# Masked cross attention: the keys of two batches projected beside the first experts, and only one token tile taken through the queries before the first maxima

## The chip, the cores and the metric

The kernel runs on one core of one Trainium2 chip. A core has TensorE (PE, matrix products), VectorE (DVE), ScalarE (ACT), GpSimd (POOL) and SyncE (SP, which here issues all transfers). The metric is the device time of one launch in microseconds; less is better.

## The reference, cut to what matters

The program is a stack of seven layers over 16 batches of 64 tokens with 128 channels. The change touches the border of the third (experts, `_L0_ffn_ref`) and the fourth (`_L1_xattn_ref`), whose first half is cross attention of 16 heads of 8 channels over 1601 context rows per batch, with an additive mask per batch and key:

```python
def _mha(x, ctx, mask, qw, qb, kw, kb, vw, vb):
    q = _split_heads(x @ qw + qb)
    k = _split_heads(ctx @ kw + kb)
    v = _split_heads(ctx @ vw + vb)
    scores = jnp.einsum('bqhd,bkhd->bhqk', q, k) / np.sqrt(D // H).astype(np.float32)
    if mask is not None:
        scores = scores + mask
    probs = jax.nn.softmax(scores, axis=-1)
    out = jnp.einsum('bhqk,bkhd->bqhd', probs, v)
...
x = x + _L0_ffn_ref(_layernorm(x, axis=-1), L0_ffn_gate, ...)
x = x + _L1_xattn_ref(_layernorm(x, axis=-1), ctx_1024, mask_Bx1x1xS2_ff0, ...)
```

The queries need `x` after the experts. Keys and values need only `ctx_1024` and the weights.

## The kernel before

Each engine has its own instruction list, written out by hand in the order in which it runs, and the lists meet at semaphores. `progress(name, steps)` makes a semaphore with named steps; `P[name].done(ins, step)` raises it, `at(engine, name, step, i)` waits for it. Every product is recorded at line 264, every tile transpose of a layer norm at line 294.

**The experts.** The first mixture of experts is a hardware loop `e0` of four iterations, two experts each. Per iteration `moe_tensor` issues for n = 0 to 3 (expert j, token half t) four steps `h` (two sums of three products of 512 columns each) and, one n later, a step `y` (16 products of 128 columns). ACT applies Silu (line 646), DVE multiplies (line 662) and adds `y` into `x` (line 667). The steps `h` use PSUM banks 0 to 3, `y` banks 4 and 5; banks 6 and 7 are free in the loop. At the start of an iteration PE waits for `wcol` (line 655), which DVE writes after the last sum.

**From the experts to attention.** After the loop DVE takes the layer norm of `x` (`ln_all_vector(3)`: statistics, variance, then 8 tiles of 128 tokens at line 277); POOL computes the reciprocal root `rstd` (line 283), behind two memsets of the value areas (lines 968 and 969). PE transposes 8 tiles and projects queries for all 1024 tokens. The queries are kept as a high and a low part, `qh` and `ql`, which lie in the same memory as `kh` and `kl`, the parts of the keys. SP copies `qh`, `ql`, `qh` into every fourth partition of `QS` (line 924). POOL spreads `QS` per batch into `QB` (line 978). Keys of a batch are projected in four chunks (512, 512, 512, 65 columns), all through PSUM bank 7: product on PE, high part on ACT (line 1081), low part on DVE (line 1493), then the next chunk. SP copies `kh`, `kh`, `kl` and the mask into the stack `KS` of that batch (lines 865, 872).

**The slots.** `slots` runs slot n = -2 to 16, each of 13 steps k. In slot n batch n has its scores and exponentials (`s`, line 1094) and weighted values, batch n+1 its values and the maxima m3 to m12 (scores over a wide tile, `maximum` on PE and a reduction on DVE, lines 1508 and 1510), batch n+2 its keys and, at k = 10 to 12, its maxima m0 to m2. `SIDES` and `MAX_STEPS` (lines 1623, 1624) say what stands at which k. Two pairs of PSUM banks take the maxima in turn. After m12 the negated maximum `nm` is transposed, split and sent by SP into `QB` (line 877, `nm_stacked`), and the batch's scores wait for that. So before slot 0 the slots -2 and -1 hold: keys of batch 0, maxima m0 to m2 of batch 0; then keys of batch 1, values of batch 0, maxima m3 to m12 of batch 0, m0 to m2 of batch 1.

## Time and profile before

| what | value |
|---|---|
| median of 3 runs | 1282.2 us (1277.72 to 1285.16) |
| the profiled execution | 1281.95 us, of it span from the first to the last instruction 1280.2 us |
| mean granted TensorE clock | 0.889 of full speed |
| PE / DVE / ACT / POOL busy | 1022.1 / 657.4 / 483.0 / 196.8 us |
| last sum of the experts | 379.4 us |
| first scores of batch 0 | 454.55 us |

The span is what the trace shows. The trace names an instruction by line, tile written and tiles read, its start and its length, and what ended the idle time before it. "PEld" is the loading of weights, "SPq" SP's issue of a transfer. A 32-bit product shows as two records, a product of `F32R` tiles as one.

### The profile page before, as it was taken

The page shows a single profiled execution, that of the slowest core. Times are in us where ns is not written, and L with a number is a line of the kernel's source. Part 1 is how long each engine was busy: PE and PEld are TensorE (multiplying, and loading weights), DVE is VectorE, ACT ScalarE, POOL GpSimd, SP SyncE. Part 2 cuts the span into 40 slices and gives each one's busy share as a digit, 9 for nine tenths or more (in the row PEclk, how much of TensorE's full clock was granted, in tenths as well). Part 3 has the DMA queues.
Part 4 walks back from the last instruction along what each step waited for, and adds up shares of the span by engine and source line. Part 5 has one row for each costly group of instructions (what it writes and reads, how often), then busy time and mean ns, then how long its engine had stood idle before and what let it go on. Part 6 is the DMA issues. An engine that isn't in the chain of part 4 may idle for free.

```text
span 1280.2 us, 22033 instructions
## 1 busy us (share of the span) xinstructions
PE 1022.1 (80%) x9278; PEld 731.4 (57%) x9278; DVE 657.4 (51%) x1131; ACT 483.0 (38%) x622; POOL 196.8 (15%) x178
## 2 busy tenths in 40 slices
PE   3687777899873699999999999999658634848888
PEld 2355456787761266666666666666436412547776
DVE  4133655343343556666666676664166367763111
ACT  0234332222232146666666656666304200402333
POOL 2000430211212001111111111110141013200110
PEclk9799887999996579999999999999877766859999
DMA  8585000101201333333333333330000100001110
GB/s 278 187 314 207 2 1 1 50 25 43 83 0 53 141 123 108 111 130 110 107 107 108 139 137 123 108 108 18 1 1 2 33 0 1 2 0 34 34 33 17
DMA packets 41349, 98.52 MB, mean 77 GB/s; under 512 B 9976, under 2 KB 24960, under 8 KB 41264
## 3 DMA queue, kind: packets, MB, share of 16 engines
q1 hardware_dynamic: 41264, 97.29, 22.1%
q8 instruction: 65, 1.06, 0.3%
q14 instruction: 20, 0.16, 0.0%
HBM read 55.50 MB, written 0.73 MB: 44 GB/s over the span
## 4 chain that ended last, share of the span: by engine, by line
PE 61%; DVE 16%; ACT 8%; issue 5%; SPq 4%; DMA 3%; POOL 3%; DVEq 0%; POOLq 0%; ACTq 0%
PE PS L264 57%; DVE kl L1493 3%; ACT kh L1081 3%; ACT PT L1094 3%; DVE prT L1497 2%; SPq L896 2%; PE PS L357 2%; DVE mx L1508 2%; DMA ctxT<-in_ctx_T 1%; PE PS L294 1%; POOL rstd_all L283 1%; DVE x L667 1%; DVE u_all L277 1%; DMA work_area<-in_ctx_T 1%; DVE stats_all L269 1%
## 5 line engine op out<-in xcount | busy, mean ns | idle before, releaser
L1508 DVE TENSOR_REDUCE mx<-PS 128x2 f32<-128x1024 f32 x192 | 230.7, 1217 | 85.1 <-PE PS L264 85.0
L1094 ACT ACTIVATE PT<-PS 128x1024 f32<-128x1024 f32 (+1 forms) x208 | 212.4, 1021 | 95.2 <-PE PS L264 94.0
L264 PE MATMUL PS<-QB,QS 128*128 128x512 f32 x576 | 159.4, 425 | 23.7 <-DVE wcol L655 21.7
L264 PE MATMUL PS<-QB,KS 128*128 128x256 f32 (+1 forms) x832 | 166.8, 323 | 9.2 <-ACT PT L1094 8.5
L264 PEld LDWEIGHTS PS<-QB,QS 128*128 128x128 f32 x576 | 110.3, 202 | 60.7 <-issue 26.8
L264 PEld LDWEIGHTS PS<-QB,KS 128*128 128x128 f32 (+1 forms) x832 | 116.5, 187 | 43.5 <-issue 31.8
L264 PE MATMUL PS<-PT,work_area 128*32 128x128 f32 (+1 forms) x3328 | 135.3, 281 | 0.5 <-ACT PT L1094 0.5
L264 PE MATMUL PS<-KS,QB 64*128 64x512 f32 (+1 forms) x512 | 110.8, 462 | 13.1 <-DMA KS<-kl 9.5
L667 DVE SCALAR_TENSOR_TENSOR x<-PS,wcol,x 128x128 f32<-128x128 f32 x128 | 44.9, 351 | 138.1 <-PE PS L264 134.7
L264 PE MATMUL PS<-nat_area,work_area 128*128 128x128 f32 (+2 forms) x1312 | 100.8, 261 | 17.2 <-DVE work_area L662 5.9
L264 PEld LDWEIGHTS PS<-nat_area,work_area 128*64 128x64 f32 (+1 forms) x1312 | 96.3, 165 | 31.3 <-ACT work_area L395 12.3
L264 PEld LDWEIGHTS PS<-PT,work_area 128*32 128x32 f32 (+1 forms) x3328 | 78.8, 109 | 46.5 <-issue 43.2
L646 ACT ACTIVATE work_area<-PS 128x512 f32<-128x512 f32 x64 | 38.3, 598 | 127.7 <-PE PS L264 127.7
L294 PE MATMUL PS<-consts,u_all 128*128 128x128 f32 x64 | 15.7, 426 | 86.6 <-DVE u_all L277 66.0
L264 PE MATMUL PS<-ctxT,w_L_xattn_ck_w 128*128 128x512 f32 (+1 forms) x128 | 66.8, 607 | 21.3 <-DVE kl L1493 17.5
L264 PE MATMUL PS<-w_L_xattn_cv_w,ctxT 128*128 128x128 f32 (+1 forms) x416 | 78.7, 311 | 0.0
L264 PEld LDWEIGHTS PS<-KS,QB 64*128 64x128 f32 x512 | 46.2, 193 | 48.9 <-issue 14.5
L1081 ACT ACTIVATE kh<-PS,c_L_xattn_ck_b 128x512 fp32r<-128x512 f32 x64 | 38.1, 595 | 86.0 <-PE PS L264 71.7
L264 PEld LDWEIGHTS PS<-w_L_xattn_cv_w,ctxT 128*128 128x128 f32 (+1 forms) x416 | 55.8, 194 | 23.3 <-issue 22.8
L1493 DVE SCALAR_TENSOR_TENSOR kl<-PS,c_L_xattn_ck_b,kh 128x512 fp32r<-128x512 f32 x64 | 40.5, 633 | 51.4 <-ACT kh L1081 51.3
L294 PEld LDWEIGHTS PS<-consts,u_all 128*128 128x128 f32 x64 | 12.5, 223 | 88.5 <-DVE u_all L277 41.0
L978 POOL TENSOR_TENSOR QB<-QS,consts 128x1024 fp32r<-128x1024 f32 x16 | 31.2, 1955 | 202.1 <-PE PS L264 186.0
(237 smaller groups left out, 1255.5 us busy)
## 6 DMA issues: line engine op xcount, KB each, us to landing
KS<-kh SPq DMA_DIRECT2D x32, 800.5 KB
ctxT<-in_ctx_T SPq DMA_DIRECT2D x24, 800.5 KB, 4.4
nat_area<-in_ctx_tiles SPq DMA_DIRECT2D x16, 832.0 KB, 6.6
KS<-kl SPq DMA_DIRECT2D x16, 800.5 KB
work_area<-in_ctx_T SPq DMA_DIRECT2D x8, 800.5 KB, 10.2
nat_area<-in_L_ffn_experts_w SPq DMA_DIRECT2D x24, 256.0 KB, 3.3
nat_area<-in_L_ffn_W SPq DMA_DIRECT2D x16, 256.0 KB, 3.0
KS<-mask_parts SPq DMA_DIRECT2D x32, 50.1 KB
```

Of the source, the lines that this page charges most:

```text
L264: return T.matmul(o, l, r, start=start, stop=stop, **k)
L294: last = T.transpose(PS[:, 512 * (6 + h) + 128 * t:512 * (6 + h) + 128 * t + 128], src[:, 4 * h + t, :], ident)
L357: last = T.transpose(PS[:, o:o + 128], L["pr"][:, 128 * b:128 * b + 128], ident)
L646: ins = S.activation(g_act[:, c % 2, :], bank(2 * (c % 2)), ACT.Silu)
L667: last = V.scalar_tensor_tensor(x[:, 4 * t + q, :], PS[:, 512 * (4 + t) + q * 128:512 * (4 + t) + (q + 1) * 128], wcol[:, j, 4 * t + q:4 * ...
L896: sp.dma_start(dst, src).then_inc(loads, 16)
L978: P["qb_g"].done(G.tensor_tensor(QB[b % 3][:, :].rearrange("p (g h q) -> p g h q", g=4, h=4), QS[:, :, SEQ * b:SEQ * b + SEQ].unsqueeze(2) ...
L1081: P["keys_a"].done(S.activation(kh[:, c0:c0 + cw], bank(7, cw), ACT.Identity, bias=COLS["L1_xattn_ck_b"][:, 0:1]), f"kh{c}")
L1094: P["exp_a"].done(S.activation(PT[0:rows, par, :], PS[0:rows, 1024:2048], ACT.Exp), f"e{k}")
L1493: P["keys_v"].done(V.scalar_tensor_tensor(kl[:, c0:c0 + cw], bank(7, cw), COLS["L1_xattn_ck_b"][:, 0:1], kh[:, c0:c0 + cw], ALU.add, ALU.s ...
L1497: P["sum_v"].done(V.reciprocal(rsum, rsum), "sum")
L1508: ins = V.reduce_max(by_pair[:, :, j // 3, j % 3:j % 3 + 1], src, AX)
```

## The change

Five things are done together.

1. **Keys in the loop.** The keys of batches 0 and 1 are projected in `e0`: 401 columns of each batch per iteration, overlapping by one column, behind step h(1, 0) for batch 0 (bank 6) and behind h(3, 0) for batch 1 (bank 7). Their contexts are loaded once the first self attention has read its tiles. Batch 1 gets parts of its own, in the early half of `nat_area`. SP stacks both behind the loop's weight loads (`stack_keys`).
2. **Values of batch 0** are projected right behind the loop, into banks 2 to 5.
3. **One tile of queries.** Only token tile 0 (batches 0 and 1) is normalised, transposed and projected first; its 128 columns go into `QS`, and the maxima of batch 0 follow. `qh` and `ql` lie in `small` and in `QB[2]`.
4. **Slots -2 and -1** keep only maxima and `nm`. The seven other tiles, and their queries, come between slot -1 and slot 0 (`q1`, `q2`); `QB` of batch 2 waits for them.
5. **Fillers.** POOL writes only the 16 one-columns of each value group, behind `rstd`; ACT fills `QS` first and `KS[2]` after `KS[1]` is stacked; `L1_xattn_co_b` is added to `u_all` on POOL.

```diff
-        qh, ql = kh[:, 0:TOKENS], kl[:, 0:TOKENS]
+        KH = [kh, nc.alloc_sbuf_tensor_at("kh1", [128, KPAD], F32R, offset=nat_at)]
+        KL = [kl, nc.alloc_sbuf_tensor_at("kl1", [128, KPAD], F32R, offset=nat_at + 4 * 1608)]
...
+        def early_keys_tensor(b, i):
+            T.wait_ge(ctxT_loaded[b], 16)
+            P["pk_p"].done(mm(bank(6 + b, KW), W["L1_xattn_ck_w"][:, :], ctxT[:, b, bass.ds((KW - 1) * i, KW)]), f"b{b}")
+
+        def early_keys_scalar(b, i):
+            at(S, "pk_p", f"b{b}", i)
+            P["pk_a"].done(S.activation(KH[b][:, bass.ds((KW - 1) * i, KW)], bank(6 + b, KW), ACT.Identity,
+                                        bias=COLS["L1_xattn_ck_b"][:, 0:1]), f"b{b}")
+
+        def early_keys_vector(b, i):
+            at(V, "pk_a", f"b{b}", i)
+            P["pk_v"].done(V.scalar_tensor_tensor(KL[b][:, bass.ds((KW - 1) * i, KW)], bank(6 + b, KW),
+                                                  COLS["L1_xattn_ck_b"][:, 0:1], KH[b][:, bass.ds((KW - 1) * i, KW)],
+                                                  ALU.add, ALU.subtract), f"b{b}")
+
+        def early_keys(keys, i):
+            return {(1, 0): lambda: keys(0, i), (3, 0): lambda: keys(1, i)}
...
+            if n < 0:
+                return [item for item in SIDES[k] if item == "nm" and n == -1]
...
+            moe_sync(sp, "e0", (A["L0_ffn_experts_w1"], A["L0_ffn_experts_w3"], A["L0_ffn_experts_w2"], None), first_contexts)
             sp.wait_ge(mask_saved, 32)
+            sp.wait_ge(stacks_ready, 2)
             for b in range(2):
-                load_context(b)
-            at(sp, "q3_v", "ql")
-            sp.wait_ge(stacks_ready, 4)
+                stack_keys(b)
+            at(sp, "q3_v", "ql0")
+            sp.wait_ge(stacks_ready, 3)
             for k, src in enumerate((qh, ql, qh)):
-                sp.dma_start(QS[k:128:4, :, :].bitcast(F32), src.bitcast(F32)).then_inc(qs_stacked, 16)
+                sp.dma_start(QS[k:128:4, :, 0:128].bitcast(F32), src[:, 0:128].bitcast(F32)).then_inc(qs_first, 16)
+            at(sp, "vals_p", "v2", 0)
+            load_context(2)
+            sync_slot(-1)
+            at(sp, "q3_v", "ql2")
+            for k, src in enumerate((qh, ql, qh)):
+                sp.dma_start(QS[k:128:4, :, 128:TOKENS].bitcast(F32), src[:, 128:TOKENS].bitcast(F32)).then_inc(qs_stacked, 16)
             slots(sync_slot)
...
-            G.memset(VA[0], 1.0).then_inc(consts_ready, 1)
-            G.memset(VA[1], 1.0).then_inc(consts_ready, 1)
             ln_all_gpsimd(3)
-            g.wait_ge(qs_stacked, 16 * 3)
+            for va in VA:
+                G.memset(va[:, :, :, 16:32], 1.0).then_inc(consts_ready, 1)
+            g.wait_ge(qs_first, 16 * 3)
...
+            def queries(j, lo, hi, src, tmp):
+                at(V, "q3_p", f"q{j}")
+                vdone(V.tensor_scalar(tmp, src, COLS["L1_xattn_cq_b"][:, 0:1], HD ** -0.5, ALU.add, ALU.mult), "q3_v", f"qf{j}")
+                vdone(V.tensor_copy(qh[:, lo:hi], tmp), "q3_v", f"qh{j}")
+                vdone(V.tensor_tensor(ql[:, lo:hi], tmp, qh[:, lo:hi], ALU.subtract), "q3_v", f"ql{j}")
+
+            ln_stats_vector(3, x)
+            ln_apply_vector(x, u_all, range(3))
+            at(V, "q3_p", "T0")
+            P["q3_v"].done(V.tensor_copy(xT_all[:, 0:128], bank(6, 128)), "x0")
+            ln_apply_vector(x, u_all, range(3, 5))
+            queries(0, 0, 128, bank(0, 128), prT[:, 512:640])
+            ln_apply_vector(x, u_all, range(5, PAIRS))
+            slot(-2)
+            slot(-1)
...
+            queries(1, 128, 512, bank(7, 384), prT[:, 512:896])
+            queries(2, 512, 1024, bank(6), prT[:, 512:1024])
             slots(slot)
```

In the rows of order below a name is that of the tile (written<-read), and the brackets name the semaphores waited for. First PE inside the loop, from the second group h(0, 2) on, as it was:

```order
L264 MATMUL PS<-QB,QS 128x512 [waits e0_v]
L264 MATMUL PS<-QB,QS 128x512 x5
L264 MATMUL PS<-nat_area,PT 128x128 [waits e0_v]
L264 MATMUL PS<-nat_area,PT 128x128 x15
L223 REGISTER_ALU
```

and as it is now, from the end of h(1, 0) to step y of n = 0:

```order
L270 MATMUL PS<-QB,QS 128x512 x5
L270 ISA [waits ctxT_loaded0]
L270 MATMUL PS<-ctxT,w_L_xattn_ck_w 128x401
L226 REGISTER_ALU
L270 MATMUL PS<-QB,QS 128x512 [waits e0_v]
L270 MATMUL PS<-QB,QS 128x512 x5
L270 MATMUL PS<-nat_area,PT 128x128 [waits e0_v]
```

One product of 401 columns stands between two steps `h`; the only wait that comes with it is that for the context.

PE behind the loop, before:

```order
L294 MATMUL PS<-consts,u_all 128x128 [waits ln_normalised,consts_ready,e0_v]
L294 MATMUL PS<-consts,u_all 128x128 x7
L264 MATMUL PS<-xT_all,w_L_xattn_cq_w 128x512 [waits ln_copied] x2
L264 MATMUL PS<-ctxT,w_L_xattn_ck_w 128x512 [waits ctxT_loaded0]
L264 MATMUL PS<-ctxT,w_L_xattn_ck_w 128x512 [waits keys_v] x2
L264 MATMUL PS<-ctxT,w_L_xattn_ck_w 128x65 [waits keys_v]
L264 MATMUL PS<-KS,QB 128x512 [waits ks_stacked0,qb_g]
```

and now:

```order
L270 MATMUL PS<-w_L_xattn_cv_w,ctxT 65x128 [waits e0_v]
L270 MATMUL PS<-w_L_xattn_cv_w,ctxT 128x128 x12
L1299 MATMUL PS<-consts,u_all 128x128 [waits ln_normalised]
L270 MATMUL PS<-xT_all,w_L_xattn_cq_w 128x128 [waits q3_v]
L270 MATMUL PS<-KS,QB 128x512 [waits qb_g,consts_ready,ks_stacked0,vals_a,q3_v]
```

The keys are gone from between the queries and the first maxima; 13 value products stand ahead of the one transpose.

PE from the end of the maxima m0 to m2 of batch 1 to the first scores (`QB,KS`), now; before, the scores followed directly on a value product and no tile or query stood here:

```order
L270 MATMUL PS<-KS,QB 128x512 [waits max_v]
L270 MATMUL PS<-KS,QB 128x512
L1402 MATMUL PS<-consts,u_all 128x128 [waits ln_normalised]
L1402 MATMUL PS<-consts,u_all 128x128 x2
L1405 MATMUL PS<-consts,u_all 128x128 x4
L270 MATMUL PS<-xT_all,w_L_xattn_cq_w 128x384 [waits ln_copied]
L270 MATMUL PS<-xT_all,w_L_xattn_cq_w 128x512 [waits ln_copied]
L270 MATMUL PS<-QB,KS 128x256 [waits nm_stacked]
```

Seven transposes and two query products now come between the last maximum and the first scores.

## Rows read from the trace of the kernel before

**Rows 1.** Head of the page.
```profile
span 1280.2 us, 22033 instructions
```

**Rows 2.** Windows: span, busy us (instructions) PE, PEld, DVE, ACT, POOL; clock, DMA share, GB/s.
```profile
379.40:424.20 44.80, 10.58 (x22) 4.57 (x22) 15.12 (x37) 11.42 (x6) 13.88 (x6) 0.61 0.26 93
424.20:454.50 30.30, 25.90 (x73) 13.06 (x73) 20.37 (x22) 4.41 (x8) 0.00 (x0) 0.50 0.24 84
454.50:480.30 25.80, 25.41 (x243) 16.60 (x241) 15.78 (x18) 14.80 (x19) 0.00 (x0) 0.87 0.38 132
480.30:506.00 25.70, 25.08 (x282) 16.48 (x281) 18.29 (x17) 15.84 (x22) 4.10 (x5) 1.00 0.37 131
```

**Rows 3.** Chain that ended last, in order: start us, us, what.
```profile
382.35 2.83 POOL work_area L969
...
398.19 4.62 DMA QS<-kh
...
406.70 2.09 PE PS L264 x2
...
416.31 7.74 DMA KS<-kl
```

**Rows 4.** Timeline from the loop's end to the first key: start us, us, engine, instruction.
```profile
379.62 1.64 DVE L269 BATCH_NORM_STATS2 stats_all<-x 128x6 f32<-128x128 f32 x8 [0.21 <-DVE x L667]
...
381.97 0.40 DVE L274 TENSOR_SCALAR var_all<-mv_all 128x8 f32<-128x8 f32 x1
...
385.14 1.63 POOL L283 TENSOR_TENSOR rstd_all<-var_all,consts 128x8 f32<-128x8 f32 x1
386.81 2.14 DVE L277 TENSOR_SCALAR u_all<-x,mv_all,rstd_all 128x128 f32<-128x128 f32 x8 [4.44 <-POOL rstd_all L283]
...
390.29 1.48 DVE L288 COPY xT_all<-PS 128x512 f32<-128x512 f32 x2 [1.34 <-PE PS L294]
...
391.03 2.93 PE L264 MATMUL PS<-xT_all,w_L_xattn_cq_w 128*128 128x512 f32 x4
...
395.59 1.23 DVE L1535 TENSOR_TENSOR kl<-PT,kh 128x1024 fp32r<-128x1024 f32 x1
...
402.84 0.69 ACT L1081 ACTIVATE kh<-PS,c_L_xattn_ck_b 128x512 fp32r<-128x512 f32 x1 [14.35 <-DMA QS<-kh]
402.88 6.58 POOL L978 TENSOR_TENSOR QB<-QS,consts 128x1024 fp32r<-128x1024 f32 x3 [16.11 <-DMA QS<-kh]
```

**Rows 5.** Timeline, maxima of batch 0 up to the first scores.
```profile
424.19 1.22 PE L264 MATMUL PS<-KS,QB 64*128 64x512 f32 x4 [9.53 <-DMA KS<-kl]
...
441.88 4.75 DVE L1508 TENSOR_REDUCE mx<-PS 128x2 f32<-128x1024 f32 x4
...
442.27 1.23 PE L264 MATMUL PS<-w_L_xattn_cv_w,ctxT 128*128 128x128 f32 x4
...
447.27 0.71 DVE L1510 TENSOR_REDUCE mx<-PS 128x8 f32<-128x528 f32 x1 [0.65 <-PE PS L264]
...
449.05 0.28 DVE L1501 TENSOR_TENSOR nml<-PS,nmh 8x128 fp32r<-8x128 f32 x1
...
454.55 1.22 PE L264 MATMUL PS<-QB,KS 128*128 128x256 f32 x4
```

**Rows 6.** Timeline inside the expert loop, last product of an iteration.
```profile
330.36 3.83 PE L264 MATMUL PS<-nat_area,work_area 128*128 128x128 f32 x32 [1.49 <-DVE work_area L662]
```

**Rows 7.** Groups by form, 229.5 to 379 us: name xcount, busy us, mean ns, idle.
```profile
L646 ACT ACTIVATE work_area<-PS 128x512 f32<-128x512 f32 x54 | 32.3, 598 | 111.1 <-PE PS L264 111.1
```

**Rows 8.** Windows of 1 us, for the granted clock (third column from the end).
```profile
389.00:390.00 1.00, 0.90 (x5) 0.94 (x6) 0.00 (x0) 0.00 (x0) 0.00 (x0) 0.50 0.00 0
...
393.00:394.00 1.00, 1.00 (x4) 0.52 (x3) 0.75 (x1) 0.00 (x0) 0.00 (x0) 1.00 0.00 0
...
450.00:451.00 1.00, 0.92 (x3) 0.52 (x4) 0.02 (x1) 0.12 (x1) 0.00 (x0) 0.50 0.02 4
...
461.00:462.00 1.00, 1.00 (x6) 0.59 (x4) 0.00 (x0) 0.33 (x1) 0.00 (x0) 0.88 0.00 0
```

More of the change, by code:

```diff
@@ L651, in moe_scalar, with moe_vector @@
                 beside.get((n, c), lambda: None)()
-        def moe_vector(name, gated, i, first=lambda: None):
+        def moe_vector(name, gated, i, first=lambda: None, beside={}):
             for j in range(2):
@@ L711, in build @@
         T_loaded = [sem(f"T_loaded{q}") for q in range(2)]
-        progress("q3_p", ["q0", "q1"])
-        progress("q3_v", ["qf0", "qf1", "qh", "ql"])
+        progress("q3_p", ["T0", "q0", "q1", "q2"])
+        progress("q3_v", ["x0"] + [f"{part}{j}" for j in range(3) for part in ("qf", "qh", "ql")])
+        progress("pk_p", ["b0", "b1"])
+        progress("pk_a", ["b0", "b1"])
+        progress("pk_v", ["b0", "b1"])
         CS = range(len(CHUNKS))
@@ L792, in slots @@
         def slots(slot):
[L794 removed]
+            for n in range(BATCH + 1):
                 slot(n)
+        KW = 401
+        def early_keys_tensor(b, i):
[12 more added lines that the diff above has]
+            return {(1, 0): lambda: keys(0, i), (3, 0): lambda: keys(1, i)}
         def maxima(n, k):
@@ L822, in bank7_free @@
         def bank7_free(n, k):
-            before = [(m, item) for m in range(-2, n + 1) for i in range(KT) for item in closed(sides(m, i))
+            before = [(m, item) for m in range(n + 1) for i in range(KT) for item in closed(sides(m, i))
                       if (m, i) < (n, k) and item != "nm"]
+            if not before:
+                at(nc.tensor, "q3_v", "ql1")
             if before:
@@ L1287, in slot @@
                             pe.wait_ge(nm_stacked, 32 * (n + 1))
+                        if n == 0 and k == 1:
+                            at(T, "q3_v", "ql2")
                         if k >= 1:
@@ L1309, in slot @@
                         maximum(b, j)
+            slot(-2)
+            slot(-1)
+            pe.wait_ge(ln_xn, 4 * PAIRS)
+            for t in range(1, 4):
+                last = T.transpose(PS[:, 3584 + 128 * (t - 1):3584 + 128 * t], u_all[:, t, :], ident)
+            last.then_inc(ln_T, 1)
+            for t in range(4, 8):
+                last = T.transpose(PS[:, 3072 + 128 * (t - 4):3200 + 128 * (t - 4)], u_all[:, t, :], ident)
+            last.then_inc(ln_T, 1)
+            pe.wait_ge(ln_xT, 7)
+            P["q3_p"].done(mm(bank(7, 384), W["L1_xattn_cq_w"][:, :], xT_all[:, 128:512]), "q1")
+            pe.wait_ge(ln_xT, 8)
+            P["q3_p"].done(mm(bank(6), W["L1_xattn_cq_w"][:, :], xT_all[:, 512:1024]), "q2")
             slots(slot)
```

125 lines of the change are left out of this document (79 added, 46 removed).

## The prediction

> **What bounds the kernel now.** I read the head of the page, then windows of the stretches around the change, then the chain that ended last, then the timeline. The span is 1280.2 us [rows 1]. From 454.5 us on, where the slots run, PE is busy 25.41 of 25.80 us and 25.08 of 25.70 us [rows 2]: the slots are bound by PE, and nothing that is only moved from one slot to another would pay. The two windows ahead look otherwise. From the end of the experts (379.4) to the first maximum (424.2) PE is busy 10.58 of 44.8 us, and no other engine more than 15.12; from there to the first scores (454.5) it is busy 25.90 of 30.3 us, but at half clock, 0.50 [rows 2]. So 75.1 us lie between the last sum of the experts and the first scores, and they are a chain of latencies: the chain holds a memset on POOL that runs until 385.2, 4.62 us for the last query transfer, 2.09 us for a product of one key chunk at half clock, 7.74 us for the stack of keys [rows 3]. This stretch is what the change is worth; the loop ahead of it is what it costs.
>
> I count from E, the last sum of the experts (379.4 before, later after), and follow PE to m0 of batch 0 and to the first scores. Before they stand at E+44.8 and E+75.1 [rows 5].
>
> **E to m0.** Statistics and variance are unchanged and end at E+3.0 [rows 4]. `rstd` then began only at 385.14, since POOL was filling [rows 3, 4]; now it is first on POOL and ends at E+3.0+1.63 = E+4.7. Of the eight tiles, 2.14 us together, three come before the transpose: E+5.5 [rows 4]. PE meanwhile does 13 value products. Two of them take 1.23 us at half clock [rows 5], so 13 take 8.0; at full clock I bound them by half of that, 4.0. Clock 1.0 holds in the loop and falls some time after PE stops, so I take the middle, 6.0: PE is free at E+6.1. Transpose, copy of 128 columns (0.74 us for 512 [rows 4]: at most 0.3), product of 128 columns (2.93 for 1024 [rows 4]: 0.5), three DVE operations on 128 columns instead of 1024 (the longest was 1.23 [rows 4]: at most 0.35 each, 0.9 with their waits) give `ql0` at E+8.4. The seven other normalised tiles fall partly in DVE's waits here, partly under the transfers.
>
> The three query transfers took 1.37 us (396.82 to 398.19) for two issues and 4.62 for the last, 6.0 us with 1024 columns [rows 3, 4]. With 128 columns the issues stay and the bytes are one eighth. No row has such a transfer on this path: it costs between its three issues alone, 2.1, and 6.0. I take the middle, 4.1: E+12.5. The Trainium skill's page "DMA: Bandwidth & Descriptors" (section on the fixed cost) gives a fixed 2.0 us and bytes over 436 kB per us; by it the last transfer would be seen 2.2 us after its issue and this term would be 3.6, the sum 0.5 less. No row here shows it.
>
> POOL then spreads one `QB`: 6.58 us for three, 2.2 each [rows 4]: E+14.7, and m0 at E+14.8. **Gone: 30.0 us.** Among them are the keys of batch 0 (four rounds of PE, ACT, DVE through one bank), their stack of 7.74 us, the co_b addition and two of the three `QB`. Their cover is safe: batch 0's last chunk is projected some 30 us before E, batch 1's some 12 us before, the stack needs some 9 us, and it is first wanted at E+14.8 and E+32.
>
> **m0 to the scores.** Before, `nml` of batch 0 ended at 449.33, 25.1 us after m0, since every other step waited for a key chunk of batch 1 [rows 5]. Now only maxima stand there: 0.8 for the first product, 12 reductions at 4.75/4 = 1.19, then 0.71 [rows 5], then the 1.35 us from there (447.98) to the end of `nml` [rows 5]: 17.2, so E+32.0. DVE sets the pace: two steps' products take 1.22 on PE [rows 5], 0.6 to 0.8 each with their start. **Gone: 8.0 us.** If instead each step's handover were seen (product and reduction in turn, 2.0 a step), it would be 10 more; with two pairs of banks the four reductions in a row at 1.19 speak against it.
>
> Behind it, 5.2 us passed to the scores; this grows. m0 to m2 of batch 1 need three reductions, 3.6: E+35.6. PE transposes seven tiles beside them. Then a copy of 384 columns, 0.6 (of 0.74 for 512), then q1 and q2 on PE: a 512-column product at half clock is 2.09 [rows 3], so 1.57+2.09 = 3.7, the second copy beside the first. Scores at E+39.9, 7.9 instead of 5.2: **added 2.7 us.** The `nm` transfers, issued from E+32 on, have 8 us to land where the query transfers took 6.0. Step k = 1 of slot 0 waits for `ql2`: three DVE operations of 512 columns, some 2 us, against scores of 1.22 [rows 5] and a maximum and a value product, together 1.2 to 1.5, on PE behind q2. Zero, 1 at worst. The other queries' transfers and `QB` of batch 2 are wanted at k = 10, some 25 us later; behind them on POOL and SP stand only work of slot 1 and the next mask. co_b on POOL has the same cover. ACT's fill of `KS[2]` moves behind its value copies and is wanted later still.
>
> So the scores come 75.1 - 39.9 = 35.2 us sooner, measured from E.
>
> **What the loop pays.** E itself moves. Eight products of 401 columns are added where PE has no idle time but 1.49 us an iteration ahead of the last step `y` and the wait for `wcol`. In the same loop 16 products of 128 columns of the same type take 3.83 us [rows 6], 0.24 each; 401 columns are 0.75. Upper bound: half of the 2.09 for 512 at half clock, 1.05 [rows 3]. Eight times 0.75 is **6.0 us**, bounds 5.8 and 8.4. ACT and DVE come along, 0.55 and 0.6 us twice an iteration (the high part of 512 columns took 0.69 [rows 4], the low part a little more). ACT had 111.1 us idle in the windows of the loop, all for PE [rows 7]. DVE's low part waits for ACT's high part, and behind it in DVE's list is the product of h(n, 1), whose reader on PE stands behind a whole step `y` of 3.83 us: hidden; without `y` it would cost some 0.5 each. An Identity on ACT after Silu shows no table load in the trace: the first `kh` at 402.84 begins with the transfer it waited for [rows 4].
>
> **Sum.** 1281.95 (the profiled execution; the median of the runs shown is 0.25 above) - 35.2 + 6.0 = 1252.8. Behind the first scores nothing changes. Forecast 1253.
>
> **Rivals.**
>
> *The clock comes back sooner, 1249.* PE began a dense stretch at 389 and the clock was 1.00 at 393; another began at 450, and it was still 0.50 until 461 [rows 8]. The forecast repeats the second: seven transposes, q1, q2 and the first scores make PE dense from about E+34, and I let slot 0 lose as much as before. If it is the first, q1, q2 and the first scores run at 2.4 GHz (2.4 us less) and some 1.5 us of slot 0 come back. The Trainium skill's page "TensorE: Matmul & The Clock Gate" (section on the two states) says that the default is throttled and sustained activity releases it; by that rule the dense stretch is what counts and this rival would hold. The first case of rows 8 agrees, the second does not, with 92% busy at 450 and half clock for 11 us.
>
> *The chain keeps part of its length, 1261.* The value products all at half clock hold the transpose 2 us longer, the transfers take their full 6.0 (1.9 more), and each maximum shows 0.3 us of handover (4 more). Each is open; together they give 8 us. For it speaks that every step of the new chain is short and waits on another engine.
>
> *The first maxima wait for something else, 1268.* The change would then not do what it says. The candidate is SP's list: the query transfers stand behind the stacks of both batches. If the last stack is issued or read so late that it is still moving at E+8, its 7.74 us come ahead of the queries, and `QB` of tile 0 is late by up to that, with the other small terms about 15 us.
>
> *The loop pays more, 1264.* PE stalls behind an inserted product until ACT and DVE have taken their parts: 0.75+0.55+0.6 and two handovers of 0.1 make 2.1 us an insertion, 17 us instead of 6. Against it: no wait on PE in the loop names the early keys but the one for the context, and the reader of the next `h` stands behind `y`.
>
> *Slower than before: the clock stays at half through the first slots, 1290.* Before, the clock rose 7 us into slot 0, and slot 0 at a mean clock of 0.87 took 25.8 us against 25.7 for the next at 1.00 [rows 2]. Now slot 0 comes after a stretch in which PE does only maxima, 0.6 of each 1.19 us, with nothing between them. If PE then stayed at 0.50, a slot with 25.1 us of PE work would grow by 0 to 25 us; with the middle, 12.5, the gain of 29 is gone after 2.3 slots, and three of them give 1253+37 = 1290. For it: the clock was 0.50 over the whole of 424 to 454 with PE busy 85% [rows 2]. Against it: it did rise, 11 us after the stretch became dense [rows 8], and slots are 97% dense.
>
> **How the numbers follow.** Forecast (1248 to 1257) 0.60, clock sooner 0.13, chain longer 0.16, something else first 0.04, loop pays more 0.03, clock at half 0.03, something not named 0.01. The range reaches over the clock rival and the longer chain, with 3 us for the spread of runs: 1245 to 1266. A measurement of this kernel tells some 0.5%, 6.4 us, from no change. Of the named cases only the clock at half ends on the other side of that, and the unnamed one may end within it or a little short: faster 0.95, same 0.02, slower 0.03.
>
> **What would show it.** In the profile after: the last sum of the experts at 385 to 386; `rstd` starting within 0.2 us of the variance; the first maximum 14 to 16 us behind the last sum; reductions of batch 0 at 1.2 us each without gaps; the first scores at 425 to 426, 40 us behind the last sum; one slot still 25.7 us. The forecast is wrong if the loop lengthens by over 9 us, if the first maximum is over 20 us behind E, or if the slots lengthen.

## The result, and the profile after

| | before | after |
|---|---|---|
| median, beside one another | 1281.39 us (1277.72 to 1285.16, 4 runs) | 1241.92 us (1235.97 to 1244.09, 4 runs) |
| repeated, same chip | 1279.8 us (11 runs) | 1240.08 us (1235.66 to 1247.4, 6 runs) |
| the profiled execution, with its clock | 1281.95 us, 0.889 | 1241.52 us, 0.908 |

The ratio is 0.9684 (95% interval 0.964 to 0.9729), and 0.9693 (0.9661 to 0.9724) in the repetition. The kernel is faster, as forecast, but by 39.5 us where 29 were forecast, and 1241.92 lies below the range of 1245 to 1266.

The head of the page of after, which answers to [rows 1], and its first line on the engines:

```profile
span 1239.7 us, 22079 instructions
...
PE 1004.5 (81%) x9280; PEld 723.3 (58%) x9280; DVE 658.4 (53%) x1136; ACT 482.1 (39%) x622; POOL 195.1 (16%) x179
```

The same line of the page of before:

```profile
PE 1022.1 (80%) x9278; PEld 731.4 (57%) x9278; DVE 657.4 (51%) x1131; ACT 483.0 (38%) x622; POOL 196.8 (15%) x178
```

PE was busy 1022.1 us before and is busy 1004.5 us now, with two records more, which is one product: eight key products came into the loop, eight left the stretch behind it, and the queries are three products instead of two. A product costs PE more time at half clock; the mean clock rose from 0.889 to 0.908. So part of the gain is not a wait that went.

Windows of after, columns as in [rows 2]: nearly all of the loop, last sum (E = 379.2) to first maximum, from there to the first scores, two slots.

```profile
204.70:379.20 174.50, 157.95 (x905) 131.56 (x904) 72.61 (x142) 46.39 (x75) 27.60 (x24) 0.98 0.18 57
379.20:394.70 15.50, 4.39 (x29) 3.63 (x30) 8.21 (x29) 11.94 (x7) 6.62 (x5) 0.73 0.18 55
394.70:417.40 22.70, 16.56 (x51) 7.73 (x51) 19.95 (x22) 0.00 (x0) 3.73 (x2) 0.51 0.02 8
417.40:443.10 25.70, 23.77 (x261) 15.55 (x259) 17.97 (x24) 14.24 (x18) 2.12 (x2) 1.00 0.44 155
443.10:468.80 25.70, 25.10 (x289) 16.63 (x282) 18.77 (x19) 15.51 (x21) 4.09 (x5) 1.00 0.38 133
```

The two stretches between loop and slots were 44.8 and 30.3 us [rows 2]; they are 15.5 and 22.7 us, together 38.2 us, 36.9 less. A slot still takes 25.7 us, but the first now runs at clock 1.00, not 0.87.

The timeline of after from E to the first maximum (start, length, engine, instruction, idle before), which answers to [rows 4]:

```profile
379.23 3.12 PE L270 MATMUL PS<-w_L_xattn_cv_w,ctxT 128*65 128x128 f32 x26 [1.60 <-DVE x L681]
...
382.06 1.63 POOL L295 TENSOR_TENSOR rstd_all<-var_all,consts 128x8 f32<-128x8 f32 x1 [39.86 <-DVE var_all L280]
...
383.64 2.91 POOL L1034 MEMSET work_area<- 128x1664 f32 x2
383.73 3.21 DVE L285 TENSOR_SCALAR u_all<-x,mv_all,rstd_all 128x128 f32<-128x128 f32 x3 [1.81 <-POOL rstd_all L295]
...
386.68 0.48 PE L1299 MATMUL PS<-consts,u_all 128*128 128x128 f32 x1 [4.33 <-DVE u_all L285]
...
389.02 0.29 DVE L1626 TENSOR_TENSOR QB<-prT,q_hi 128x128 fp32r<-128x128 f32 x1
389.34 0.53 SPq L982 DMA_DIRECT2D QS<-q_hi  x1
...
392.56 3.74 POOL L1044 TENSOR_TENSOR QB<-QS,consts 128x1024 fp32r<-128x1024 f32 x2 [6.02 <-DMA QS<-q_hi]
...
394.71 1.22 PE L270 MATMUL PS<-KS,QB 64*128 64x512 f32 x4 [6.38 <-POOL QB L1044]
```

And from the last reductions of batch 0 to the first scores, which answers to [rows 5]:

```profile
409.98 0.18 DVE L1609 TENSOR_REDUCE nm<-mx 128x8 f32<-128x32 f32 x1
...
411.01 0.28 DVE L1596 TENSOR_TENSOR nml<-PS,nmh 8x128 fp32r<-8x128 f32 x1
...
415.44 2.50 PE L270 MATMUL PS<-xT_all,w_L_xattn_cq_w 128*128 128x384 f32 x4 [0.24 <-DVE xT_all L1638]
...
417.38 1.03 PE L270 MATMUL PS<-QB,KS 128*128 128x256 f32 x4
...
420.75 0.50 PE L270 MATMUL PS<-QB,KS 128*128 128x256 f32 x2 [1.54 <-DVE QB L1626]
```

**Where the 40.5 us between the two spans went.** I cut both traces at four points: start of the experts' loop (first copy to `wcol`), start of the layer norm behind it, first exponential of batch 0, first exponential of batch 15.

| stretch | before | after | difference |
|---|---|---|---|
| launch to the loop | 204.2 | 200.6 | -3.6 |
| the loop | 175.4 | 178.8 | +3.4 |
| its end to the first exponential | 76.2 | 39.1 | -37.1 |
| first to last batch's exponentials | 437.2 | 436.4 | -0.8 |
| to the end | 387.2 | 384.9 | -2.3 |

The forecast had +6.0, -35.2 and nothing else. Three things are therefore to be explained: the loop pays less, the chain loses more, and over 5 us come from the first and the last stretch, in which no work of an engine was changed (ahead of the loop only SP's loads of two contexts were added).

In the last stretch PE has 2148 records in both traces and is busy 264.89 us before and 262.88 after: 2.0 of the 2.3 us. In the first it has 1234 in both and is busy 133.96 and 133.08 us: 0.9 of the 3.6. So PE's own slower running accounts for most of the last difference, and not for the first.

### The profile page after: what moved, and what is told of

Read it like the earlier page. It is cut to its first block, busy times and chain, and to the rows that moved or that the text cites. A ratio compares the mean times of both kernels' runs of the same rounds, so it can differ in the third digit from the quotient of the medians.

```text
span 1239.7 us, 22079 instructions
## 1 busy us (share of the span) xinstructions
PE 1004.5 (81%) x9280; PEld 723.3 (58%) x9280; DVE 658.4 (53%) x1136; ACT 482.1 (39%) x622; POOL 195.1 (16%) x179
## 4 chain that ended last, share of the span: by engine, by line
PE 60%; DVE 18%; ACT 8%; issue 5%; SPq 4%; POOL 3%; DMA 2%; DVEq 0%; POOLq 0%; ACTq 0%
PE PS L270 56%; ACT PT L1170 3%; DVE kl L1588 3%; DVE mx L1603 3%; ACT kh L1157 2%; DVE prT L1592 2%; SPq L948 2%; PE PS L369 2%; DMA ctxT<-in_ctx_T 1%; POOL rstd_all L295 1%; PE PS L306 1%; DVE x L681 1%; DVE u_all L285 1%; DVE stats_all L275 1%; DMA work_area<-in_ctx_T 1%
## 5 line engine op out<-in xcount | busy, mean ns | idle before, releaser
L270 PE MATMUL PS<-w_L_xattn_cv_w,ctxT 128*128 128x128 f32 (+1 forms) x416 | 73.7, 299 | 1.6 <-DVE x L681 1.6
L270 PEld LDWEIGHTS PS<-w_L_xattn_cv_w,ctxT 128*128 128x128 f32 (+1 forms) x416 | 52.8, 186 | 22.6 <-issue 20.6
L270 PE MATMUL PS<-ctxT,w_L_xattn_ck_w 128*128 128x512 f32 (+2 forms) x128 | 60.1, 551 | 3.8
L270 PEld LDWEIGHTS PS<-nat_area,PT 128*128 128x128 f32 x512 | 61.2, 196 | 1.4
L270 PE MATMUL PS<-nat_area,PT 128*128 128x128 f32 x512 | 61.5, 280 | 0.0
L580 POOL TENSOR_TENSOR QS<-nat_area,consts 128x512 fp32r<-128x512 f32 x24 | 25.0, 1040 | 225.0 <-DMA nat_area<-in_L_ffn_experts_w 125.9
```

Of the source, the lines that this page charges most:

```text
L270: return T.matmul(o, l, r, start=start, stop=stop, **k)
L580: P[name + "_g"].done(G.tensor_tensor(hi, w[:, j, :], one.broadcast_to([128, FF]), ALU.mult), f"w{2 * k + 1}hi{j}")
```

## The experiments

The theory: the changed stretch is worth 34 to 35 us whatever the execution; the rest is the time that untouched stretches spend at half clock, which comes out otherwise when the program ahead of them gets longer or shorter. The rival: the change itself makes other stretches shorter (a queue or a buffer that is free sooner). Beside these stand questions on single terms.

### Both kernels again: what repeats

**before_again**, the kernel before, unchanged.

> The kernel before once more, unchanged, for its stretches outside the changed code. In the two traces so far 3.6 us of the difference lie ahead of the expert loop (start of the loop 204.2 against 200.6 us) and some 3.3 us behind the first scores, all of it in stretches with 6.8 and 13 us less time at half clock; the fifteen full slots agree to 0.1 us. Theory phase: these 7 us are not the change's, and a second trace of the same program gives other shares of half clock: loop start anywhere in 200 to 205, from exp 15 to the end within 4 us of 387.2. Theory change: the change itself moves them, and this trace repeats 204.2 for the start of the loop and 387.2 from exp 15 to the end, within 0.7 us each.

**after_again**, the changed kernel, unchanged.

> The changed kernel once more, unchanged, five rounds. Theory phase: start of the loop differs from 200.6 by 1 us or more, and the sum of both outer stretches moves toward the ones of before; the ratio stands nearer to what the changed stretch alone gives, (1281.4-33.5)/1281.4 = 0.974. Theory change: loop start 200.6 and the end stretch of 384.9 repeated within 0.7 us, ratio 0.968. In both the stretch from the end of the loop to the first scores is 38.2 us within 1 us, and an insertion in the loop costs 0.67 us.

| | before | before_again | after | after_again | after_third (below) |
|---|---|---|---|---|---|
| launch to the loop | 204.2 | 205.2 | 200.6 | 204.9 | 199.8 |
| loop to first exponential | 251.6 | 251.5 | 217.9 | 217.8 | 217.5 |
| last batch to the end | 387.2 | 387.5 | 384.9 | 383.7 | 388.0 |

The changed stretch repeats within 0.4 us: 33.8 us gained, and with slot 0 (30.72 to 30.02 us) 34.5. The start of the loop does not repeat: 204.9 in after_again. The 3.6 us ahead of the loop in the first pair were chance. What sets the start is open. The last stretch repeats in before (387.2, 387.5) and varies in after (383.7 to 388.0). The expectation of before_again says 13 us less at half clock behind the first scores; the two traces hold 146.7 and 136.7 us, so it is 10. before_again is a single execution, of 1282.99 us.

### The memsets of POOL ahead of `rstd`

The timeline above has a row that no term of the sum foresaw: three tiles of the norm take 3.21 us. The answer for line 285 in after gives shortest, median and longest of the eight:

```profile
L285 DVE TENSOR_SCALAR u_all<-x,mv_all,rstd_all x8: 328/343/2896, 383.7 to 389.9; 128x128 f32<-128x128 f32 x8
```

The first ran 2.90 us beside POOL's two memsets, which began 0.09 us before it. Theory: the memsets hold it. **fill_first** moves them ahead of `rstd`.

```diff
-            ln_all_gpsimd(3)
             for va in VA:
                 G.memset(va[:, :, :, 16:32], 1.0).then_inc(consts_ready, 1)
+            ln_all_gpsimd(3)
```

> The changed kernel with POOL's two memsets of the one-columns ahead of rstd instead of behind it. In the trace of the changed kernel the first of DVE's normalised tiles took 2.90 us where the others take 0.33, exactly while POOL ran its two memsets (383.64 to 386.55), and PE waited for that tile. Theory collision: a memset on POOL holds up that DVE instruction; with the memsets in the 2.9 us in which POOL is idle anyway (379.2 to 382.1) the first tile takes 0.33 us and everything behind comes 2.6 us sooner: 2.6 us faster, ratio about 0.002 under that of the changed kernel. Theory wait: the long tile is the profile's way to show a late rstd; then nothing is gained, or rstd comes later by what the memsets overrun and the kernel is 0 to 0.3 us slower.

Timeline of fill_first:

```profile
379.27 2.91 POOL L1033 MEMSET work_area<- 128x1664 f32 x2 [37.30 <-DVE x L681]
...
382.29 1.63 POOL L295 TENSOR_TENSOR rstd_all<-var_all,consts 128x8 f32<-128x8 f32 x1
...
383.96 0.86 DVE L285 TENSOR_SCALAR u_all<-x,mv_all,rstd_all 128x128 f32<-128x128 f32 x3 [1.75 <-POOL rstd_all L295]
384.36 0.33 PE L1299 MATMUL PS<-consts,u_all 128*128 128x128 f32 x1 [1.98 <-DVE u_all L285]
...
391.92 1.22 PE L270 MATMUL PS<-KS,QB 64*128 64x512 f32 x4 [6.36 <-POOL QB L1044]
```

`rstd` starts 0.23 us later, three tiles take 0.86 us, and the first maximum comes 2.8 us sooner. That the memsets held the tile is shown. The Trainium skill, page "SBUF — State Buffer" (section "Who interferes with whom"), says that GpSimd and a VectorE `tensor_scalar` in a two-port mode take one shared pair of ports by turns, each for its whole instruction. The trace agrees in kind, though here the tile ended with the second of two memsets, not the first. That this `tensor_scalar` ran in such a mode no row shows.

Measured whole: 1240.6 us (6 runs), ratio 0.9715 (0.9688 to 0.9741), against 1240.08 for after_again. The 2.8 us are not to be seen there, so it was timed again beside the changed kernel, on another chip, as **fill_first_again** and **after_third**.

> The changed kernel a third time, as the yardstick of the two kernels that follow on the same chip. It was 1240.1 and 1241.9 us; within 1238 to 1243. In its trace the tile held up by POOL's memsets takes 2.9 us again, and the first scores stand 38.2 us behind the end of the loop.

> The kernel with POOL's memsets ahead of rstd again, since five rounds could not tell 2.6 us (its trace showed nm of batch 0 at 27.8 instead of 30.6 us behind the end of the loop, its median was 0.5 us above the changed kernel's). Theory collision: 1 to 4 us faster than the changed kernel on the same chip, and the first tile at 0.33 us. Theory nothing gained: what is won ahead of the slots is given back by the clock behind them, and the medians stay within 1 us.

1243.86 us (1242.49 to 1245.4) for the changed kernel, 1242.15 us (1235.78 to 1244.43) for fill_first: 1.7 us less, with overlapping runs and ratios of 0.9722 (0.9693 to 0.9752) and 0.971 (0.9681 to 0.974). The gain is real in the stretch (28.1 us to `nm` of batch 0 against 30.6), and not resolved in the whole.

### What an inserted key product costs

**keys_twice** issues each key product in the loop twice.

```diff
             T.wait_ge(ctxT_loaded[b], 16)
+            mm(bank(6 + b, KW), W["L1_xattn_ck_w"][:, :], ctxT[:, b, bass.ds((KW - 1) * i, KW)])
             P["pk_p"].done(mm(bank(6 + b, KW), ...
```

> The changed kernel with each of the eight inserted key products issued twice into the same bank, the second overwriting the first: same result, eight products of 401 columns more in the loop. Theory PE bound: each adds 0.67 us, the four iterations grow by 5.4 us in all, up to 1.7 us more or less for each half-clock stretch gained or lost. Theory hidden: the insertions cost the loop only 3.4 us in all because part of them falls into waits, and eight more add under 2 us. Nothing else moves.

The insertion for batch 0 in the first iteration, on PE's timeline, in after and then in keys_twice:

```profile
210.43 0.83 PE L270 MATMUL PS<-ctxT,w_L_xattn_ck_w 128*128 x2
```

```profile
210.33 1.51 PE L270 MATMUL PS<-ctxT,w_L_xattn_ck_w 128*128 x4
```

One more product is 0.68 us. Eight would be 5.4, but the loop grew by 4.0 us only (178.8 to 182.8); the single execution took 1248.29 us. The iterations tell why. Windows of the third one, before, after and keys_twice:

```profile
292.30:336.30 44.00, 39.54 (x224) 33.02 (x224) 16.98 (x35) 10.86 (x17) 9.20 (x8) 0.96 0.12 35
```

```profile
291.00:334.70 43.70, 39.26 (x228) 32.71 (x228) 18.22 (x37) 12.04 (x19) 9.20 (x8) 1.00 0.12 36
```

```profile
292.20:338.50 46.30, 41.92 (x232) 34.64 (x232) 18.23 (x36) 12.04 (x19) 9.19 (x8) 0.96 0.11 33
```

In after this iteration has four records more and is shorter than before: its clock is 1.00, where before it was 0.96. In keys_twice, the clock is 0.96 again and the iteration 2.6 us longer, for two products that cost 1.35. An iteration has one short stretch at half clock, which begins about where PE waits for `wcol`, or it has none. Over the loop, half clock sums to 14.6 us before, 11.5 in after, 8.1 in keys_twice. What one such stretch costs can be read from after_delay (a run described below, with the same loop), where the third iteration has it:

```profile
299.70:344.70 45.00, 40.61 (x228) 33.77 (x228) 18.24 (x36) 12.06 (x19) 9.21 (x8) 0.96 0.12 35
```

That is 1.3 us more than in after, for the same 228 records. So the loop pays 3.4 us, and would pay about 4.7 with as many half-clock stretches as before. fill_first_again bears this out: its loop has 14.4 us at half clock and takes 179.8 us, 4.4 more than before. Of the 5.4 us that eight products cost by keys_twice, the clock gives back about 1.3, and 0.7 are hidden in some other way, which no run separates.

### One tile first, or all eight

**all_tiles** keeps all of the change but item 3: all tiles and queries come before the maxima, and whole rows go into `QS`.

```diff
-            at(sp, "q3_v", "ql0")
+            at(sp, "q3_v", "ql2")
...
-                sp.dma_start(QS[k:128:4, :, 0:128].bitcast(F32), src[:, 0:128].bitcast(F32)).then_inc(qs_first, 16)
+                sp.dma_start(QS[k:128:4, :, :].bitcast(F32), src.bitcast(F32)).then_inc(qs_first, 16)
...
-            slot(-2)
-            slot(-1)
             P["q3_p"].done(mm(bank(6), W["L1_xattn_cq_w"][:, :], xT_all[:, 512:1024]), "q2")
+            slot(-2)
+            slot(-1)
```

> The changed kernel with one part undone: all eight token tiles are normalised, transposed and projected before the first maxima, and QS is sent in three full transfers, as before; keys in the loop, values and fillers stay. Theory (the chain as the prediction built it): seven transposes, one copy, q1, q2 and three DVE operations of 512 columns, some 8 us, and 2.8 us more for full transfers come ahead of m0, and some 1.5 us fall away between nml and the scores: the scores stand 9 to 10 us later, at E+47 to 48, ratio 0.007 above the changed kernel's. Rival: PE, DVE and POOL would have waited anyway and only the longer transfer counts: 3 us.

Timeline of all_tiles; E is 377.0 there:

```profile
395.12 0.53 SPq L982 DMA_DIRECT2D QS<-q_hi  x1
...
401.55 3.74 POOL L1039 TENSOR_TENSOR QB<-QS,consts 128x1024 fp32r<-128x1024 f32 x2 [17.19 <-DMA QS<-q_hi]
403.50 1.22 PE L270 MATMUL PS<-KS,QB 64*128 64x512 f32 x4 [10.45 <-POOL QB L1039]
```

The transfers take 6.4 us with all columns (6.0 before, 3.2 with one tile), the first maximum is at E+26.5 instead of E+15.5, the first exponential 7.5 us later than in after: of the 11 us, 3.5 come back since no tile and query stand between slots -1 and 0. Whole: 1251.76 us (1245.53 to 1255.13), ratio 0.9794 (0.9762 to 0.9826). The first scores stand at E+45.5, 7.3 us behind those of after, where 9 to 10 were expected: the delay ahead of the first maximum is as expected, but more of it comes back. Item 3 is worth 7.5 us in the stretch, and 8 to 12 between the medians.

### Keys in the loop, or behind it

**keys_after** takes the eight key products out of the loop and puts them, with their parts on ACT and DVE, right behind it. On PE:

```diff
-                moe_tensor("e0", True, i, early_keys(early_keys_tensor, i))
+                moe_tensor("e0", True, i)
             pe.wait_ge(P["e0_v"].sem, 4 * P["e0_v"].n)
+            for i in range(4):
+                for b in range(2):
+                    if i:
+                        at(T, "pk_v", f"b{b}", i - 1)
+                    early_keys_tensor(b, i)
```

> The changed kernel with another part undone: the eight key products of batches 0 and 1, with their high and low parts, stand right behind the loop instead of in it, through banks 6 and 7 in turn; the rest stays. Theory: the loop is 5.4 us shorter (eight times 0.67), but the eight products, the stacks of 2.4 MB for each batch (7.7 us behind the last low part) and the query transfers queued behind them come ahead of m0: m0 at E+26 to 30 instead of E+15.5, the kernel 6 to 9 us slower than the changed one. Rival: the stack of batch 0 alone counts and the queries slip past it; then m0 at E+19 and the kernel is 2 us faster or the same.

Timeline of keys_after; E is 375.5 there:

```profile
385.06 1.31 DVE L829 SCALAR_TENSOR_TENSOR kl<-PS,c_L_xattn_ck_b,kh 128x401 fp32r<-128x401 f32 x2 [0.99 <-ACT kh L824]
...
394.29 1.48 SPq L982 DMA_DIRECT2D QS<-q_hi  x1
...
403.34 5.54 ACT L1136 ACTIVATE KS<-consts 128x6408 fp32r<-128x6408 f32 x1 [12.53 <-DMA KS<-kl]
403.98 3.74 POOL L1044 TENSOR_TENSOR QB<-QS,consts 128x1024 fp32r<-128x1024 f32 x2 [21.09 <-DMA QS<-q_hi]
```

The keys themselves are done at E+10.9. The query parts were ready at 389.9, but their transfers are issued at 394.29, behind the stacks of both batches on SP, and land 9.7 us later where after needs 3.2. The loop is 3.4 us shorter, the chain to the first exponential 15.8 us longer (54.8 against 39.1). Whole: 1250.65 us (1250.1 to 1252.47), ratio 0.978 (0.9754 to 0.9807). So keys in the loop are worth 12.4 us by the trace and 7 to 11 between the medians. The first maximum comes 15.1 us later behind E (406.13, E+30.6). Of this the query parts are 4.3 us later, their issue waits 4.4 us behind SP's issues for the stacks, and their landing takes 6.5 us more: ACT's fill, which waits for the stack of batch 1, begins only at 403.34. So 10.9 of the 15.1 us are not PE's work but the stacks ahead of the queries. This is the prediction's rival "something else first", brought about.

### Does the clock bound the new chain?

The clock is 0.73 and 0.51 in the two stretches of the new chain. **warm_fill** is fill_first with spare products, whose results are not used: 16 behind the values, 20 behind the first queries, two behind each maximum of batch 0.

```diff
+            spare(16)
             pe.wait_ge(ln_xn, 3 * PAIRS + 1)
...
             pe.wait_ge(consts_ready, 3)
+            spare(20)
...
                 P["max_p"].done(last, f"m{j}")
+                if b == 0:
+                    spare(2)
```

> fill_first with spare products on PE where it would wait: 16 of 128 columns behind the values, 20 behind the first query product, 2 behind each maximum of batch 0, all into bank 7, which nobody reads then. Nothing is left out. Theory clock: the clock stays at full from the end of the loop to slot 0, which shortens the transpose, q0, the products of m0 and nm, the seven transposes, q1 and q2: nm of batch 0 some 1 us sooner, the first scores 2 to 2.5 us sooner than in fill_first. Rival: the spare products themselves stand ahead of what PE is waited for (two per maximum, 0.5 to 1 us each step if the clock does not rise), the steps go from 1.13 to over 1.3 us, and the kernel is 1 to 4 us slower.

The clock stayed at full until `nm` of batch 0, and nothing was won: from the start of the norm to `nm` 28.5 us, against 27.8 and 28.1 in the two traces of fill_first, where 1 us less was expected. The first scores came at E+36.4, against E+35.1 and E+36.1. Two rows of fill_first, then two of warm_fill:

```profile
394.03 0.80 PE L270 MATMUL PS<-KS,QB 64*128 64x512 f32 x2 [0.89 <-DVE mx L1603]
...
412.66 2.22 PE L270 MATMUL PS<-xT_all,w_L_xattn_cq_w 128*128 128x384 f32 x4 [0.24 <-DVE xT_all L1638]
```

```profile
396.55 0.49 PE L270 MATMUL PS<-KS,QB 64*128 64x512 f32 x2 [0.41 <-POOL QB L1044]
...
416.66 3.36 PE L270 MATMUL PS<-xT_all,w_L_xattn_cq_w 128*128 128x384 f32 x4 [0.24 <-DVE xT_all L1647]
```

The two products of a maximum take 0.49 us instead of 0.80, and the step from one maximum to the next is 1.07 to 1.13 us against 1.13 all the same, since DVE's reduction sets it. The 16 spare products also outlasted the norm and held the transpose by some 1.5 us; without that, 1 us or a little more would be left as a gain (an estimate from the three traces). And the clock, full for so long, fell for the query products: 3.36 us where fill_first has 2.22 and after 2.50. Whole: 1243.57 us (1236.78 to 1248.06), against 1242.15 for fill_first on the same chip. By this estimate the half clock costs this chain about 1 us, and keeping it away in this way costs as much.

### Do untouched stretches answer to a shift?

Take the stretch from the norm at the end of this layer's cross attention to the norm behind the next attention, whose instructions are the same in both kernels. Its window, in before, after and after_third:

```profile
931.10:998.50 67.40, 47.22 (x488) 32.67 (x488) 43.31 (x73) 17.15 (x17) 16.70 (x9) 0.75 0.07 17
```

```profile
891.50:955.30 63.80, 43.61 (x488) 29.90 (x488) 43.28 (x72) 17.14 (x17) 16.69 (x9) 0.81 0.08 18
```

```profile
892.00:959.50 67.50, 47.32 (x488) 32.50 (x488) 43.31 (x73) 17.14 (x17) 16.69 (x9) 0.75 0.06 17
```

488 products each, DVE busy 43.3 us each, and 3.6 us between them: PE is busy 3.6 us less where the clock is 0.81. after and after_third are the same program. Some of it comes back at once: the next stretch, up to the norm behind it, takes 29.5 us in after and 28.4 in after_third, so the two together differ by 2.6 us. If the place of the stretch against the clock's turns decides, a shift of 1 to 2 us ahead of it must do in the kernel before what the change seemed to do. **before_delay** adds two idle copies on DVE ahead of the norm, to the kernel before; **after_delay** adds three to the changed kernel. They were meant as 1.4 and 2.1 us. A copy takes 0.69 us, but the next instruction starts 0.60 us behind it, so in the traces they move the norm by 1.2 and 1.8 us.

```diff
             at(V, "l1_p", "cy")
+            V.tensor_copy(PT[:, 0, :], xT_all[:, :])
+            V.tensor_copy(PT[:, 1, :], xT_all[:, :])
```

> The kernel before with two such copies at the same place (1.4 us on the path). Theory fall of the clock: the same stretch takes 63.8 instead of 67.4 us, so that 1.4 us of added work make the kernel about 2 us faster, and the 3.3 us that the changed kernel gained behind the first scores are seen without the change. Theory change: the stretch stays 67.4 and the kernel is 1.4 us slower.

> The changed kernel with three copies of 1024 columns into free tiles on DVE ahead of the layer norm that ends the cross attention (0.69 us each, 2.1 us in all, on the path). Everything else is the same. The stretch from that norm to the norm behind the next attention took 67.4 us in both traces of the kernel before and in the one with the key products twice (34.1 us at half clock), and 63.8 in three traces of the changed kernel (23.9 us at half clock). Theory fall of the clock: which of the two it is depends only on when the stretch begins against the clock's own steps, so moving it by 2.1 us gives 67.4 here, and the kernel is 2.1+3.6 us longer. Theory change: the shorter stretch belongs to the changed program, and it stays 63.8.

The stretch took 63.9 us in before_delay, as expected, and 64.4 us in after_delay, which is neither value and against the expectation of 67.4. The single executions took 1274.29 and 1251.58 us. Both were then timed over several executions, as **before_delay_timed** and **after_delay_timed**.

> The kernel before with 1.4 us of copies ahead of the norm at the end of the cross attention, now timed. The runs of the kernel before show a mean clock of 0.887 to 0.889 in eight of eleven cases, the changed kernel's anything from 0.901 to 0.911; in two traces of before the stretch behind the norm took 67.4 us, in the one with the copies 63.9. Theory lock: the kernel before reaches this stretch at nearly the same point of the clock's steps in most runs, an unlucky one, and the copies move it away: median 1 to 4 us faster than before although it does more, mean clock above 0.889. Theory chance: in the mean of runs the point is random for both kernels, and the copies cost what they take: 1 to 2 us slower.

> The changed kernel with 2.1 us of such copies, timed. Theory lock: the changed kernel's point is luckier, the copies spend that, and it is 3 to 5 us slower than the changed kernel's 1240 to 1244, ratio 0.973 to 0.975. Theory chance: 2 us slower, ratio 0.971 to 0.973; the two lie too near for this run alone.

The window in before_delay_timed:

```profile
930.30:994.20 63.90, 43.65 (x488) 29.91 (x488) 43.27 (x73) 17.14 (x17) 16.70 (x9) 0.79 0.07 18
```

With 1.2 us more to do the kernel took 1275.97 us (12 runs) against 1278.54 (17 runs) for the kernel before, ratio 0.9971 (0.9957 to 0.9986): 3.7 us less by the ratio, 2.6 by the medians. Work was added and time went, with nothing that could be free sooner. This speaks for the theory and against the rival, at least for an effect of this size in these stretches. The other way round it did not come out in size: after_delay_timed took 1249.71 us (1244.18 to 1250.79, 6 runs), 6 to 10 us above the three medians of the changed kernel for 1.8 us of work, more than either theory had. Its profiled execution has the stretch at 67.5 us, but that execution is the shortest of the six, 1244.18 us; the five of 1248.4 to 1250.8 us have no trace. The trace of after_delay, at 1251.58 us, shows where a long execution of this program can lose time: its loop begins at 209.3 us instead of 200.6, so 8.7 of the 10.1 us above after lie ahead of the loop, where neither the change nor the copies can reach. Over all fifteen traces of this case the loop begins between 198.6 and 209.3 us.

## Why the prediction was right or wrong

**What held.** The diagnosis: two stretches of waits between loop and slots, of which the keys' rounds, their stack and the whole-width queries could go. The first maximum at E+15.5 (14 to 16 named), reductions at 1.14 us without gaps, a slot at 25.7 us. Of the named signs two missed: the last sum came at 379.2, not 385 to 386 (the loop began 3.6 us sooner by chance and grew by 3.4 only); the first scores stood at 417.4, E+38.2, not at 425 to 426. `rstd` began 0.15 us behind the variance as named, but the tile that it released did not run at once.

**The chain, 36.9 us gained instead of 35.2.** Step by step:

| step | predicted | measured in after |
|---|---|---|
| `rstd` ends | E+4.7 | E+4.5 |
| 13 values done | E+6.1 | E+3.2, all at full clock |
| first tile ready | E+5.5 (three tiles) | E+7.4, held by the memsets |
| `ql0` done | E+8.4 | E+10.1 |
| the transfers | 4.1 | 3.2 |
| `QB` | 2.2 | 1.9 |
| m0 | E+14.8 | E+15.5 |
| m0 to the end of `nml` | 17.2 | 16.6 |
| `nml` to the scores | 7.9 | 6.1 |
| wait for `ql2` in slot 0 | 0 to 1 | 1.5 |

Two terms were mis-sized against each other. The values were put at 6.0 us, the middle between the clocks; the clock was full until they were done, and they took 3.1 us, less than the 4.0 that was the bound for full clock. That bound was half of what two products alone take at half clock (1.23 us), but in a row a product takes 0.24 us, as [rows 6] already had it (3.83 us for 16). And the edit "fillers behind `rstd`" was costed only as what it takes from POOL's list, never as what POOL's memset does to DVE while it runs: 2.6 us that fill_first gives back. The maxima took 16.6 us instead of 17.2, since a reduction came every 1.14 us and not every 1.19. For the transfers, issue to landing of the last was 1.93 us in the chain of after, and the term 3.2. The Trainium skill, page "DMA: Bandwidth & Descriptors" (section "Anatomy of one DMA — SWDGE (gpsimd) path"), has a fixed 2.0 us and bytes over 436 kB per us; the prediction's estimate of 3.6 us from it came nearer than my middle of 4.1.

**The clock rival.** I gave 0.13 to a clock that comes back by the first scores. It did: windows of 1 us in after, around the last query product and the scores.

```profile
416.00:417.00 1.00, 1.00 (x3) 0.45 (x2) 0.00 (x0) 0.00 (x0) 1.00 (x1) 0.53 0.00 0
...
418.00:419.00 1.00, 1.00 (x8) 0.58 (x6) 0.93 (x3) 0.55 (x1) 0.00 (x0) 1.00 0.00 0
```

Of [rows 8] the first case repeats, not the second. It gave 1.2 us on q1 and q2 (2.50 instead of 3.7) and 0.7 in slot 0, of the 4 that I had priced; the wait for `ql2` took some of it. Its figure of 1249 was still 7 us too high, for the reasons of the other terms. The slower rival (half clock in the slots) did not happen at all: 1.00 from 417.4 on.

**The loop, 3.4 us instead of 6.0.** The price of a product was right in kind, 0.67 measured against 0.75 taken, and eight of them, 5.4, lie a little below the lower bound of 5.8, for which the prediction shows no working. The missing step is that the sum took the loop's clock as given. It lost one of its stretches at half clock, worth about 1.3 us. Another 0.7 us of the products did not show in the loop; where they are hidden is open.

**"Behind the first scores nothing changes."** This is the sentence that failed, with its silent other half, that nothing changes ahead of the loop. In the first pair it cost 3.6 us ahead and 2.3 behind. Ahead, the repetition shows chance. Behind, the medians of three chips differ by 39.5, 39.7 and 36.9 us where the changed stretch and slot 0 give 34.5: 2.4 to 5.2 us more come from stretches that the change did not touch. This excess is only just clear of noise: 34.5 us alone would be a ratio of 0.9731, which lies just above two of the three intervals (up to 0.9729 and 0.9724) and inside the third (0.9693 to 0.9752). That a shift alone can take some 3 us from such stretches is shown by before_delay_timed. That it is the whole of the rest is argued, not shown, and after_delay_timed says that my picture of it is not complete: the time ahead of the loop varies by more than the excess, and why it does is open.

**The sum with what was measured:** 1281.95 + 3.4 - 37.1 - 0.8 = 1247.5 for the changed stretch and the slots, inside the range; the 5.9 us from untouched stretches make it the 1241.5 of the profiled execution. The forecast erred by 5.3 us in its own terms (2.6 in the loop, 1.9 in the chain, 0.8 in the slots) and by 5.9 in what it took for fixed. The range had 3 us for the spread of runs and nothing for the second.

## What to carry to other kernels

A stretch in which each engine waits for the next is priced step by step, and the steps to look at twice are those where another engine runs beside it: a memset moved off one engine's path landed on another's, and a queue's order (stacks ahead of queries) was worth more than the products moved. Where a program has many short idle times of PE, the half-clock time of stretches that are not edited is no constant (136.7 to 143.6 us in the last stretch of three traces of after): allow a few us for it, on both sides, and don't read the difference of one pair of traces as the change's own work. Filling PE's idle time with spare products pays nothing where another engine sets the step.

## What was not expected of the hardware

- A `tensor_scalar` of 128x128 on DVE took 2896 ns beside two memsets on POOL, and 0.33 to 0.35 us otherwise.
- The same 488 products, with the same work on DVE, took 63.8 or 67.5 us in two executions of one program, at granted clocks of 0.81 and 0.75; adding copies that move the work by 1.2 us made a kernel 0.3% faster (0.9971, 0.9957 to 0.9986).
- Half clock hardly slowed the step from one maximum to the next: 1.13 us at half clock, 1.07 to 1.13 at full, with DVE's reduction as the bound.
- Three transfers into every fourth partition took 3.2 us with 128 columns and 6.4 with 1024, but 9.7 behind the stacks of two batches.
